# A gather-and-sum graph kernel: memsets behind the gathers dropped, GpSimd's lead limited, bank clearing moved to ScalarE

## The reference, cut to what matters

```python
def _rgcn_layer(x, W, SW, b, src, dst, rel):          # twice
    xt = jnp.einsum('nd,rde->rne', x, W)
    msg = xt[rel, src]
    agg = jax.ops.segment_sum(msg, dst, num_segments=x.shape[0])
    return jax.nn.relu(agg + x @ SW + b)
...
deg = jax.ops.segment_sum(jnp.ones_like(dst, dtype=jnp.float32), dst, num_segments=N)
d_invsqrt = jnp.maximum(deg, 1.0) ** (-0.5)
d_invsqrt = d_invsqrt[:, None]
feat = jax.nn.relu(x @ W1 + b1)
h = feat * d_invsqrt
agg = jax.ops.segment_sum(h[src], dst, num_segments=N)
feat = feat - agg * d_invsqrt
return feat @ W2 + b2
```

## Time and profile before

| | |
|---|---|
| median of 3 runs | 7342.03 us (7341.99 to 7355.17) |
| span of the profiled execution | 7320.2 us |
| GpSimd busy | 5851.5 us, 80% |
| TensorE busy, matmuls | 3691.2 us, 50% |
| VectorE busy | 1720.1 us, 23% |
| ScalarE busy | 409.6 us, 6% |
| granted TensorE clock, mean | 0.636 of full |
| DMA, over the span | 52 GB/s |

### The profile page before, as it was taken

How to read it: one execution, slowest core, us unless ns; L and a number is a source line. 1 busy time by engine, 2 the same in 40 slices (tenths; PEclk the granted TensorE clock), 3 DMA queues, 4 the chain that set the end, 5 groups by cost and what they waited for, 6 DMA issues and landing times.

```text
span 7320.2 us, 56431 instructions
## 1 busy us (share of the span) xinstructions
PE 3691.2 (50%) x13687; PEld 2669.6 (36%) x13841; DVE 1720.1 (23%) x2844; ACT 409.6 (6%) x915; POOL 5851.5 (80%) x9940
## 2 busy tenths in 40 slices
PE   4555555555555556556565555554424333433343
PEld 3333333333333333334343333433323333333333
DVE  4333333333333212222222222221101111111111
ACT  1000000000000100000000000010000000000000
POOL 7888888888888588888888888867888888888887
PEclk7666667676666777767677776675555555555555
DMA  2111111111111112211222221211111111111111
GB/s 66 49 51 52 50 50 50 51 52 50 50 52 51 40 49 57 56 56 55 56 58 56 56 57 56 56 54 42 51 51 52 51 51 51 51 51 53 51 51 48
DMA packets 197585, 382.88 MB, mean 52 GB/s; under 512 B 84322, under 2 KB 93326, under 8 KB 197542
## 3 DMA queue, kind: packets, MB, share of 16 engines
q0 software_dynamic: 159456, 326.88, 17.0%
q1 hardware_dynamic: 36416, 54.67, 2.1%
q10 hardware_dynamic: 1670, 0.85, 0.0%
HBM read 356.43 MB, written 25.65 MB: 52 GB/s over the span
## 4 chain that ended last, share of the span: by engine, by line
POOL 48%; issue 20%; another core or an unknown queue 20%; PE 7%; DVE 3%; DVEq 1%; POOLq 0%; ACT 0%; DMA 0%; ACTq 0%; SPq 0%
POOL rows L794 39%; POOL pause L798 9%; PE bank L980 3%; PE bank L950 3%; DVE r_S L1042 1%; DVE r_hot L1037 1%; PE bank L1205 1%; ACT r_agg L904 0%; PE bank L1440 0%; PE bank L964 0%; DVE acc L1081 0%; DMA acc<-in_dst_dram 0%; DVEq L1071 0%; POOLq L109 0%
## 5 line engine op out<-in xcount | busy, mean ns | idle before, releaser
L794 POOL DMA_INDIRECT rows<-in_x_dram,idx x1661 | 1588.6, 956 | 466.9 <-issue 396.7
L794 POOL DMA_INDIRECT rows<-x_d,idx x1647 | 1574.2, 956 | 453.5 <-issue 397.8
L794 POOL DMA_INDIRECT rows<-h_d,idx x1640 | 1566.9, 955 | 441.4 <-issue 396.3
L980 PE MATMUL bank<-r_S,rows 128*128 128x128 f32 x6644 | 1408.2, 380 | 705.1 <-issue 486.8
L1205 PE MATMUL bank<-r_S,rows 128*128 128x64 f32 x3322 | 821.9, 388 | 1332.3 <-issue 1079.4
L980 PEld LDWEIGHTS bank<-r_S,rows 128*128 128x128 f32 x6644 | 1299.5, 285 | 501.4 <-issue 482.1
L1205 PEld LDWEIGHTS bank<-r_S,rows 128*128 128x128 f32 x3322 | 775.1, 315 | 1378.0 <-issue 1272.4
L798 POOL MEMSET pause<- 128x128 f32 x4948 | 1096.3, 222 | 4.3 <-issue 0.2
L1042 DVE TENSOR_TENSOR r_S<-bank,key 128x1792 f32<-128x1792 f32 x238 | 480.4, 2019 | 1225.9 <-remote 1080.3
L964 PEld LDWEIGHTS bank<-zeros_bf 128*128 128x128 bf16 x476 | 54.1, 114 | 1463.0 <-issue 1056.8
L964 PE MATMUL bank<-zeros_bf 128*128 128x512 bf16 x323 | 174.9, 542 | 722.4 <-issue 505.8
(11 more groups left out here) (152 smaller groups left out, 1471.1 us busy)
## 6 DMA issues: line engine op xcount, KB each, us to landing
rows<-in_x_dram,idx POOLq DMA_INDIRECT x1661, 3.3
rows<-x_d,idx POOLq DMA_INDIRECT x1647, 3.4
rows<-h_d,idx POOLq DMA_INDIRECT x1640, 3.4
d_xr<-in_x_dram SPq DMA_DIRECT2D x54, 218.0 KB
x_d<-d_yr SPq DMA_DIRECT2D x27, 218.0 KB
d_x1r<-x_d SPq DMA_DIRECT2D x27, 218.0 KB
h_d<-d_hr SPq DMA_DIRECT2D x27, 218.0 KB
part_d<-d_pr SPq DMA_DIRECT2D x27, 218.0 KB
```

Of the source, the lines that this page charges most:

```text
L794: pool.indirect_dma_start(out=self.c.rows[:, self.place(s), :], out_offset=None, in_=self.table[:, :], in_offset=bass.IndirectOffsetOnAxis ...
L980: mm = pe.matmul(agg_ps[j][:, bass.ds(offs[j * KG + k], TK)], c.rows[:, g.place(h * KG + k), :], S[:, pb, j * KG + k, :], start=False, sto ...
```

## The change

Four things are changed. GpSimd's memsets and the semaphore `paused` are gone. From a round's second iteration on, GpSimd waits for the sum of the pair two before and not four before (`LEAD`); in the first iteration it waits between pairs until the last group of the pair before has landed (`breathe`). TensorE's clearing matmul is gone: ScalarE clears the bank after it has copied it out, behind a wait for the copy, and only then gives it back. And the counts take one matmul of 96 columns per group in place of three of 32, so that `found` has 96 partitions and its turning into degrees takes twelve accumulating matmuls in place of four transposes.

```diff
+LEAD = 2
...
-        c.pause = sb("pause", [P, PT, P])
-        c.found = sb("found", [NODES, DEG_COLS + COLS])
+        c.found = sb("found", [SPOTS, DEG_COLS + COLS])
...
-        self.rest = PAIR if then is None else 1
...
+    def breathe(self, pool, i, p):
+        pool.wait_ge(self.landed[p * PAIR - 1], (i + 1) * (KG * 16))
+        gate(pool, self.c.passed)
+
     def run(self, pool, ready, stored):
...
-        def iteration(q, i, part, set_of, skip=0):
+        def iteration(q, i, part, set_of, skip=0, first=False):
             at = set_of * UN
             for p in part.pairs:
...
-                pool.wait_ge(self.summed, self.pairs_summed(q, i, p))
+                ahead = PR if first else LEAD
+                pool.wait_ge(self.summed, self.pairs_summed(q, i, p + PR - ahead))
                 gate(pool, self.c.passed)
+                if first and p > 0:
+                    self.breathe(pool, i, p)
                 for h in range(p * PAIR, (p + 1) * PAIR):
-                    if h % rest == 0:
-                        pool.wait_ge(self.paused, q * (NG // rest) + i * (RING // rest) + h // rest + 1)
-                        gate(pool, self.c.passed)
                     for k in range(part.of(h)):
...
-                        ins = pool.memset(self.c.pause[:, s % PT, :], 0.0)
-                    if h % rest == rest - 1:
-                        ins.then_inc(self.paused, 1)
...
                     act.copy(agg[:, h, :, :], agg_ps[h % BUFS][:, :].rearrange("p (n r) -> p n r", r=NREL)
-                             ).then_inc(agg_out, 1)
+                             ).then_inc(taken, 1)
+                    act.wait_ge(taken, n + (h + 1))
+                    zero(act, c, agg_ps[h % BUFS][:, :]).then_inc(agg_out, 1)
...
                     pe.wait_ge(agg_out, n + (h + 1))
-                    pe.matmul(agg_ps[j][:, :], c.zeros_bf[:, :], c.zeros, start=True, stop=False,
-                              skip_group_check=True)
...
                             for of in range(PAIR):
-                                for b in range(COLS):
-                                    at = of * COLS + b
-                                    mm = pe.matmul(cnt_ps[:, at:at + 1],
-                                                   placed[:, pb, of, b * NODES:(b + 1) * NODES], c.one_bf[:, :],
-                                                   start=True, stop=True)
+                                mm = pe.matmul(cnt_ps[:, of:of + 1], placed[:, pb, of, :], c.one_bf[:, :],
+                                               start=True, stop=True)
...
-                        window = c.found[:, bass.ds(blocks_at[first + j], COLS)]
-                        ins = dve.tensor_tensor(window, window, cnt_ps[:, j * COLS:(j + 1) * COLS], ALU.add)
+                        window = c.found[:, bass.ds(blocks_at[first + j] + (COLS - 1), 1)]
+                        ins = dve.tensor_tensor(window, window, cnt_ps[:, j:j + 1], ALU.add)
...
-            mm = pe.transpose(self.PD[:, b * NODES:(b + 1) * NODES], c.found[:, b * DEG_ROWS:(b + 1) * DEG_ROWS],
-                              c.ident[0:NODES, 0:NODES])
+            for o in range(COLS):
+                at = b * DEG_ROWS + COLS - 1 - o
+                mm = pe.matmul(self.PD[:, b * NODES:(b + 1) * NODES], c.found[:, at:at + DEG_ROWS],
+                               c.ident[0:SPOTS, o * NODES:(o + 1) * NODES], start=(o == 0), stop=(o == COLS - 1))
```

More of the change, by code:

```diff
@@ L137, in build @@
         c.zeros_bf = sb("zeros_bf", [P, P], BF16)
-        c.zeros = c.zeros_bf[:, 0:1].broadcast_to([P, BANK])
         c.one_bf = sb("one_bf", [P, 1], BF16)
@@ L707, in __init__ @@
         self.cleared = sem("cleared")
-        self.paused = sem("paused")
         self.idx_ready = sem("idx_ready")
@@ L767, in early @@
             ).then_inc(then.landed[t // KG], 16)
+    def breathe(self, pool, i, p):
+        pool.wait_ge(self.landed[p * PAIR - 1], (i + 1) * (KG * 16))
+        gate(pool, self.c.passed)
     def run(self, pool, ready, stored):
-        rest = self.rest
-        def iteration(q, i, part, set_of, skip=0):
+        def iteration(q, i, part, set_of, skip=0, first=False):
             at = set_of * UN
@@ L776, in iteration @@
                 if (p + 1) * PT <= skip:
-                    pool.sem_inc(self.paused, PAIR // rest)
                     continue
                 pool.wait_ge(self.idx_ready, (q * (IT + 1) + i) * PR + p + 1)
-                pool.wait_ge(self.summed, self.pairs_summed(q, i, p))
+                ahead = PR if first else LEAD
+                pool.wait_ge(self.summed, self.pairs_summed(q, i, p + PR - ahead))
                 gate(pool, self.c.passed)
+                if first and p > 0:
+                    self.breathe(pool, i, p)
                 for h in range(p * PAIR, (p + 1) * PAIR):
-                    if (h + 1) * KG <= skip:
-                        if h % rest == rest - 1:
-                            pool.sem_inc(self.paused, 1)
-                        continue
-                    if h % rest == 0:
-                        pool.wait_ge(self.paused, q * (NG // rest) + i * (RING // rest) + h // rest + 1)
-                        gate(pool, self.c.passed)
                     for k in range(part.of(h)):
@@ L797, in iteration @@
                         ).then_inc(self.landed[slot], 16)
-                        ins = pool.memset(self.c.pause[:, s % PT, :], 0.0)
-                    if h % rest == rest - 1:
-                        ins.then_inc(self.paused, 1)
         def one_round(q, skip=0):
-            iteration(q, 0, FULL, 0, skip)
+            iteration(q, 0, FULL, 0, skip, True)
             with pool.Fori(0, IT // SETS) as n:
@@ L828, in run @@
         pool.end_ifs()
-        pool.wait_ge(self.paused, rounds * (NG // rest) + 1)
-        gate(pool, self.c.passed)
         if self.then is not None:
@@ L864, in relational_sum @@
     agg_out = sem("agg_out")
+    taken = sem("taken")
     mixed = sem("mixed")
@@ L871, in relational_sum @@
     zeroed, zeros = prologue.zeroed if prologue else sem("zeroed"), 2
-    agg_ps, mix_ps, cnt_ps = c.psum[0:2], c.psum[2], c.psum[5][0:NODES, 0:PAIR * COLS]
+    agg_ps, mix_ps, cnt_ps = c.psum[0:2], c.psum[2], c.psum[5][0:SPOTS, 0:PAIR]
     NIT = 1 + IT + ENDS
@@ L893, in scalar @@
             early.zero(act, g, zeroed)
+        for b in range(BUFS):
+            zero(act, c, agg_ps[b][:, :]).then_inc(agg_out, 1)
         rounds = rounds_of(act, c, 0, most)
@@ L1016, in vector @@
         dve.sem_inc(added, 1)
-        dve.sem_inc(agg_out, BUFS)
         dve.sem_inc(tallied, 1)
```

## The result

The changed kernel takes 7379.82 us (median of 4, 7373.86 to 7397.44), the kernel before 7344.53 us beside it (4 runs): ratio 1.005, interval 1.0034 to 1.0066. It is 0.5% slower where 7135 us and 3% faster were forecast.

A forecast was written before the change was run, and what follows sets the result against it. GpSimd was taken as the bound, TensorE nearly level. Gathers with stops - 277 us, stage starts + 72, ends - 10 + 7: - 208 from the median of 7342.03, so 7135 us; own range 7000 to 7290, 8-in-10 range 6590 to 7480.

The forecast's parts named there:

- A pair of bare gathers takes 14 x 1.251 us: GpSimd's gathers without memsets: 1.251 us from one to the next, so 17.5 us a pair.
- The remaining waits are free: GpSimd's waits left in each pair cost zero; up to 0.64 us a pair (221 us) kept for the range.
- Stops at the lead of two: GpSimd waiting for the sum two pairs back: 18.7 us a pair in stage 3, 19.7 in stages 1 and 2.
- The break-even of 2.46 us a pair: GpSimd's stops per pair above which the change is slower: 19.96 us a pair in all.
- it stays as it is: Rival: GpSimd's stops at the limit come to 2.46 us a pair, 7340 us; chance 0.07.
- something common sets it: Reason for no difference: all three stages run at 20.0 to 20.3 us a pair although their stops differ.
- GpSimd's steady stream slows TensorE, and a stop frees it: TensorE crawls while GpSimd's gathers and memsets stream; a GpSimd stop of some 3 us frees it.
- A quick TensorE: Rival: TensorE is quick once the memsets are gone, so GpSimd hardly stops: 6600 us; chance 0.20.
- the 6494 of its bare sum: Quick TensorE without stops, 345 pairs x 17.5 us: 7342 - 920 + 72 = 6494 us.
- the starts: Starts of the three stages: pair 4 must wait for the sum of pair 2, + 29 + 29 + 14 = + 72 us.
- TensorE's relief and ScalarE's clears: Fewer TensorE matmuls, 4.3 us an iteration, off GpSimd's path; ScalarE's 476 more clears add + 4 us at stage ends.
- The profile stands 21.8 us under the median, which I keep: Profiled span of 7320.2 us against the median of 7342.03; the difference was kept in the forecast.

The follow-up runs named there:

- e19_half_mm: The changed kernel with every second matmul of each group's sum left out (4 of 7 tiles summed): 7378.52 us.
- e4_light: The changed kernel with GpSimd's part of the kernel before (memsets, `paused`, lead of four) put back: 7136.41 us, ratio 1.000 to the kernel before.
- e6_before: The kernel before, unaltered, run again for its trace: 7136.5 us.
- e10_nowrites: The kernel before without its memsets, waits at group ends kept on a plain semaphore count: 7551.33 us against 7230.26 us, ratio 1.045.

## Why the prediction was wrong, point by point

- *A pair of bare gathers takes 14 x 1.251 us.* Right, in both conditions: 1.249 to 1.252 us at the median in all traces without memsets. With no stops it is 17.48 us a pair.
- *The remaining waits are free.* Right: 0.30 us at a met wait, in every run.
- *Stops at the lead of two.* The mechanism was right (released by TensorE, several us each), the size was not, and this is the step that failed. I let one stop of 3.7 us free TensorE for three pairs, 1.2 us a pair in stage 3, and put 2.2 in stages 1 and 2. Measured late: mostly one of some 5.7 us behind every second pair. GpSimd is idle 3.06, 3.38 and 2.78 us on average ahead of a pair, 0.30 of it the usual gap, and the pairs take 2.90, 3.23 and 2.62 us more than 17.51. The break-even of 2.46 us a pair was set right, and the rival "it stays as it is", 7340 us, comes nearest; I gave it 0.07. Its reason, "something common sets it", fits `e19_half_mm`, which keeps its 20 to 20.7 us a pair with fewer matmuls. What the common thing is stays open.
- *"GpSimd's steady stream slows TensorE, and a stop frees it"*, read from the earlier trace rows: for the late condition right only in part. Its completions come later than its recorded work, and of those after 302 of 511 are seen in a stop. That the memsets slow it is refuted: late, the kernel without them is the slower one by 2.6 to 4.5%.
- *"A quick TensorE", 6600 us.* It is what the change does on time: 6315 us, some 180 below the 6494 of its bare sum. Of these, 58 are the starts, which I took at + 72 us (on time + 12, + 2 and 0; late + 25, + 9 and + 11), and 95 are the stages' starts and ends of the kernel before, 362 us late and 267 on time. Another 20 are the difference of span and median, which I had kept (below). The range of 6590 to 7480 holds the time first measured, 7380 us, but not this one.
- *TensorE's relief and ScalarE's clears are near nothing.* Right on time (`e4_light`, 1.000); late not tried alone.
- *The profile stands 21.8 us under the median, which I keep.* Wrong: the profiled run after took 7397.44 us with a span of 7395.6. Span and time differ by 2 us; the profiled execution before was simply a quicker one.
- *The trace was taken for the kernel's.* The deepest error: nothing in the prediction asks whether the slow TensorE belongs to the kernel or to the condition of the run; it forecast 7135 us from late rows, and neither condition gives it. Two things in the trace before spoke for the latter: 20% of the chain under "another core or an unknown queue" (0% in `e6_before`), and additions released by "remote" 4 us behind the last recorded matmul, which by count was of the pair after theirs.

## What to carry to other kernels

Where waiting engines are released long after the recorded end of the work that they wait for, compare the semaphore's rise with that end before building on the trace: if they are apart, busy shares and matmul counts say nothing of TensorE, and taking work from it (here 3 of 7 matmuls) may bring nothing. Count the rises as well: where most are missing, as late, the recording itself is a suspect. A change that removes pacing from the engine that bounds a kernel can be worth 11.5% in one condition and cost 0.5% in another; what decided here was not how many stops there were but that they came to about 3 us a pair. Measure such a change more than once, on several chips and at several times.

## What the runs showed of the hardware

Late and on time are not properties of a single chip: chip 6 ran the kernel before in 7135.85 and later in 7230.26 us (no trace of it; the one beside it, `e10_nowrites`, is late), chip 9 in 7146.81 and later in 7340.26. The late condition costs the kernel before, whose 222 ns writes and waits pace GpSimd at 19.5 to 20.2 us a pair on time, 1.3 to 2.9%; the changed kernel 17% (7382.85 against 6315.36 us); and the one without writes and with a lead of four 20% (7534.51 and 7551.33 against 6284.45 us, one run). So the kernel that is quickest on time is the slowest late, and neither of the two without writes that were met in both conditions beats the kernel before in both.
